# Moving the late expert-weight pieces of an audio tower: one beside each sampling chunk, sixteen into the attention's second stage

## The reference

```python
h = tok(x)                                   # 3 spliced frames -> 128 features, 166 tokens a sequence
h = h + linear_recurrence(layernorm(h))      # 256 complex states
h = h + mixture0(layernorm(h))               # 16 experts, top 2; per-expert mean of silu(x w1), then w2
h = h + sparse_attention(layernorm(h))       # 8 heads; 38 sampled keys choose 25 queries a head
h = h + mixture1(layernorm(h))               # 64 experts, top 42; gelu(x w1 + b1) w2 + b2, weighted sum
```

## Time and profile before

| | before |
|---|---|
| median of 3 runs | 2065.45 us (2064.77 to 2066.51) |
| the profiled execution | 2067.39 us |
| its span | 2065.7 us |
| PE busy | 1870.1 us (91%) |
| DVE busy | 1676.4 us (81%) |
| ACT busy | 1378.0 us (67%) |
| POOL busy | 1455.0 us (70%) |
| mean granted clock of PE | 0.939 |

### The profile page before, as it was taken

The page is one execution under the profiler, slowest core; times in us unless marked ns, Lnnn a source line. Parts: engine busy times, 40 slices in busy tenths (PEclk is TensorE's granted clock), DMA queues, the critical chain, the costliest instruction groups (busy, mean ns, idle before and its releaser), DMA issues.

```text
span 2065.7 us, 50535 instructions
## 1 busy us (share of the span) xinstructions
PE 1870.1 (91%) x17038; PEld 1349.7 (65%) x17038; DVE 1676.4 (81%) x4833; ACT 1378.0 (67%) x2149; POOL 1455.0 (70%) x1098
## 2 busy tenths in 40 slices
PE   7887436789989978999999999999999999999998
PEld 5555213456669855777777777777777777777776
DVE  5887736555678788899999999999999999999998
ACT  4134525424435545888888888888888888888886
POOL 2216679559800032888888888888888888888887
PEclk9998768789989965999999999999999999999999
DMA  3011289523200010000000200000100000000000
GB/s 93 21 35 63 81 246 257 124 67 94 90 1 1 22 63 1 2 2 0 0 0 3 82 2 0 0 0 35 49 1 0 0 0 2 2 10 11 10 11 19
DMA packets 64334, 77.56 MB, mean 38 GB/s; under 512 B 38932, under 2 KB 47028, under 8 KB 62132
## 3 DMA queue, kind: packets, MB, share of 16 engines
q1 hardware_dynamic: 61364, 70.08, 11.7%
q0 software_dynamic: 2816, 5.45, 0.8%
HBM read 42.97 MB, written 24.08 MB: 32 GB/s over the span
## 4 chain that ended last, share of the span: by engine, by line
PE 58%; DVE 3%; issue 2%; ACT 1%; POOL 0%; ACTq 0%; DVEq 0%; POOLq 0%
PE bank L2679 30%; PE bank L2662 28%; DVE m_work L2553 1%; DVE m_best L2550 1%; DVE m_work L2544 0%; PE bank L2632 0%; DVE m_ut L1269 0%; ACT m_h L2485 0%; DVE m_best L2543 0%; DVE m_ex L2555 0%; DVE h L2591 0%; DVE m_red L2556 0%; DVE m_row L2536 0%; POOL m_diag L1255 0%; ACT m_hidden L2482 0%
## 5 line engine op out<-in xcount | busy, mean ns | idle before, releaser
L2679 PEld LDWEIGHTS bank<-weights,m_h 128*128 128x128 f16 x10752 | 649.6, 98 | 194.4 <-DVE hc L2582 82.6
L2430 POOL TENSOR_TENSOR m_h<-m_hidden,m_h 128x896 f16<-128x896 f32 x384 | 725.9, 1890 | 32.0
L2679 PE MATMUL bank<-weights,m_h 128*128 128x128 f16 x10752 | 724.6, 219 | 10.7 <-POOL m_h L2430 2.1
L2582 DVE SCALAR_TENSOR_TENSOR hc<-bank,m_shares,hc 128x128 f32<-128x128 f32 x2688 | 727.2, 342 | 4.3 <-PE bank L2679 4.3
L2482 ACT ACTIVATE m_hidden<-bank,m_b 128x896 f32<-128x896 f32 x384 | 386.9, 1007 | 197.6 <-PE bank L2662 197.5
L2567 DVE TENSOR_TENSOR m_h<-bank,m_h 128x896 f16<-128x896 f32 x384 | 419.2, 1092 | 116.8 <-ACT m_h L2485 116.7
L2428 POOL TENSOR_SCALAR m_h<-m_hidden 128x896 f16<-128x896 f32 x384 | 360.8, 939 | 117.9 <-ACT m_hidden L2482 99.5
L2662 PE MATMUL bank<-m_u_first,weights 128*128 128x448 f16 (+1 forms) x1536 | 417.8, 354 | 5.5 <-DVE h L2591 5.5
L2662 PE MATMUL bank<-m_u_second,weights 128*128 128x448 f16 (+1 forms) x1536 | 417.7, 354 | 0.0
L2479 ACT ACTIVATE bank<-bank,m_b 128x896 f32<-128x896 f32 x384 | 377.6, 983 | 0.6 <-PE bank L2662 0.6
L2485 ACT ACTIVATE m_h<-bank 128x896 f16<-128x896 f32 x384 | 349.1, 909 | 0.0
(11 more groups left out here) (359 smaller groups left out, 2153.9 us busy)
## 6 DMA issues: line engine op xcount, KB each, us to landing
weights<-expert_factors SPq DMA_DIRECT2D x12, 1024.0 KB, 8.8
lru_w_in<-e_w_dram SPq DMA_DIRECT2D x16, 512.0 KB, 4.5
expert_factors<-lru_w_out SPq DMA_DIRECT2D x16, 512.0 KB, 4.3
ew_raw<-e_w_dram SPq DMA_DIRECT2D x16, 512.0 KB, 3.9
weights<-w_dram SPq DMA_DIRECT2D x16, 256.0 KB, 2.8
weights<-w_dram SPq DMA_DIRECT2D x4, 1024.0 KB, 6.6
expert_factors<-ew_made SPq DMA_DIRECT2D x8, 512.0 KB, 3.0
xs<-x_dram SPq DMA_DIRECT2D x4, 996.0 KB, 11.8
```

What stands on the lines that cost most here:

```text
L2430: g.tensor_tensor(h1[:, x, 1], hidden[:, x], h1[:, x, 0], ALU.subtract).then_inc(second_of[1], 1)
L2582: last = v.scalar_tensor_tensor(acc[:, m * TW:(m + 1) * TW], y[q][:, (n - start) * TW:(n - start + 1) * TW], shares[:, m, e:e + 1], acc[:, ...
L2679: last = t.matmul(y[q][:, (n - start) * TW:(n - start + 1) * TW], factors[:, m, n * TW:(n + 1) * TW], k.weights[:, grp % 2, 2 + m, at], st ...
```

## The change

All 32 pieces go to `ExpertWeights`; `LateWeights` is gone, and with it its SP and POOL instructions in the tiles, its 16 loads and 16 stores there, and its semaphores. The two small sums of the first mixture (`hsum`, `ym`) move to the front of their room.

- Pieces 0 to 15 stand in the first attention stage: piece c-1 after diagonal c for c = 1 to 15, and piece 15 after them, ahead of POOL's constants for the second stage. Nothing stands ahead of the first diagonal.
- Pieces 16 to 31 stand in `attend`, where SP and POOL get instructions: SP loads and stores, POOL 64 operations. SP's last wait for the stores moves there.

```diff
@@ FirstMixture
-        late.sync_load(sp, 0)
-        late.sync_load(sp, 1)
...
-            if j >= self.KEEP_FROM and (j - self.KEEP_FROM) % self.KEEP_EVERY in (0, 2):
-                late.sync_keep(sp)
-        while late.kept < late.count:
-            late.sync_keep(sp)
-        late.sync_kept(sp)
...
-    def pool(self, pool):
-        for i in range(self.late.count):
-            self.late.pool_piece(pool, i)
@@ sparse_attention, first stage
-                k.expert_weights.sync_pieces(sp, *PIECES_N3)
                 k.expert_weights.sync_pieces(sp, *PIECES_SAMPLE)
...
-                k.expert_weights.pool_pieces(pool, *PIECES_N3)
                 first, end = PIECES_SAMPLE
                 for c in range(NC):
                     norm.pool_diagonal(pool, c, c % 2, stats)
-                    if 1 <= c <= end - first:
+                    if c:
                         k.expert_weights.pool_pieces(pool, first + c - 1, first + c)
+                k.expert_weights.pool_pieces(pool, first + NC - 1, end)
@@ attend
+        @block.sync
+        def _(sp):
+            k.expert_weights.sync_pieces(sp, *PIECES_ATTEND)
+
+        @block.gpsimd
+        def _(pool):
+            k.expert_weights.pool_pieces(pool, *PIECES_ATTEND)
+
@@ constants and ExpertWeights.sync_pieces
-PIECES_N3, PIECES_SAMPLE, PIECES_SENDING = (0, 3), (3, 2 * GROUP), (2 * GROUP, NG * GROUP)
+PIECES_SAMPLE, PIECES_ATTEND = (0, 2 * GROUP), (2 * GROUP, NG * GROUP)
...
-        if end == 2 * GROUP:
+        if end == NG * GROUP:
             for p in range(2):
-                sp.wait_ge(self.k.kept_out[p], 16 * GROUP // 2)
+                sp.wait_ge(self.k.kept_out[p], 16 * (NG - 1) * GROUP // 2)
```

More of the change, by code:

```diff
@@ L937, in recurrence @@
         routing.begin(ctx, on_diag[:], tables.work[:], va[:], raw_room)
-        mixture = FirstMixture(nc, k, routing, w_in[:], w_out[:], ut[:], state_of[:], xc[:], xsn[:])
+        mixture = FirstMixture(nc, k, routing, ut[:], state_of[:], xc[:], xsn[:])
         diag_ready = sem("diag_ready")
@@ L992, in _ @@
             mixture.pool_clear(pool)
-            mixture.pool(pool)
         @block.scalar
@@ L1281, with __init__ @@
     W2_AT = (3, 8, 13)
-    KEEP_FROM, KEEP_EVERY = 4, 5
-    def __init__(self, nc, k, routing, w_in, w_out, ut, state_of, xc, xsn):
+    def __init__(self, nc, k, routing, ut, state_of, xc, xsn):
         def sem(name):
@@ L1289, in __init__ @@
         states = state_of.rearrange("p a b c d e -> p (a b c d e)")
[L1290 to L1294, removed]
+        self.hsum = states[:, 0:FC * E0 * E0].rearrange("p (f x) -> p f x", f=FC)
+        self.ym = states[:, FC * E0 * E0:FC * E0 * E0 + 128]
         self.part = xc.rearrange("p q c -> p (q c)")[:, 0:NST * FC].rearrange("p (n f) -> p n f", f=FC)
@@ L1329, in sync @@
     def sync(self, sp, outputs_made):
-        k, routing, late = self.k, self.routing, self.late
+        k, routing = self.k, self.routing
         sp.wait_ge(outputs_made, NC)
-        late.sync_load(sp, 0)
-        late.sync_load(sp, 1)
         sp.wait_ge(k.w0_split, NC)
@@ L2210, in pool_pieces @@
             g.tensor_tensor(out[:, 1], left, out[:, 0], ALU.add).then_inc(self.split, 1)
[L2215 to L2264, removed]
-            pool.wait_ge(self.kept_out[j], 16 * (i // 2))
-        g.tensor_copy(out[:, 0], raw).then_inc(self.rounded, 1)
-        pool.wait_ge(self.rounded, i + 1)
-        if i:
-            pool.wait_ge(self.split, i)
-        g.tensor_tensor(left, raw, out[:, 0], ALU.subtract).then_inc(self.raw_read, 1)
-        pool.wait_ge(self.raw_read, i + 1)
-        g.tensor_scalar(left, left, 1.0 / SHARE, 1.0, ALU.mult, ALU.mult).then_inc(self.widened, 1)
-        pool.wait_ge(self.widened, i + 1)
-        g.tensor_tensor(out[:, 1], left, out[:, 0], ALU.add).then_inc(self.split, 1)
```

## The result

The changed kernel takes 2071.87 us, the median of 15 runs (2066.66 to 2076.78). The kernel before takes 2064.43 us (15 runs, 2062.63 to 2066.96). The ratio is 1.0033, with a 95% interval of 1.0022 to 1.0043: slower, by 7.4 us. That is a third of a per cent, clear of the noise by its interval. The forecast was 2078.

What follows compares the result with a forecast made beforehand. POOL was taken to pace the tiles through SP's waits, PE to bound the sampling and be fullest in the attention's second stage. 2067.4 - 25 - 10 + 48 = 2080.4, less 1.9 for the median: 2078 us, range 2060 to 2098.

Steps and rivals of the forecast that it cites:

- The tiles, -25: First mixture's tiles: without SP's waits for POOL, DVE becomes the limit; 25 us less, bounds 0 and -36.
- The third norm, -10: Third norm and sampling: PE's wait for the first diagonal, DVE's waits and the low clock go; -10 us, bounds -5 and -12.
- The 3 us for the clock: Third norm: at full clock PE's 11.0 busy us shrink by some 4, of which ACT's copies give back 1.
- Sampling, 0: Sampling chunks: PE covers the pieces; DVE's numbering of heads meets POOL at work, 0 to 3 us, taken as 0.
- The second stage, +48: Attention's second stage: DVE waits for POOL's operations, steps of 6.85 us instead of 3.7; +48 us, bounds +40 and +60.
- the 0.06 us for each of four holds: Second stage: DVE's holds add about 0.06 us to each of four POOL operations, making a 6.6 us piece 6.85.
- A step that starts otherwise falls into that order: Second stage: steps settle with POOL's long operations in DVE's gaps, so four operations, one piece, go with each step.
- The second mixture as long as before: Second mixture: its length was expected to stay unchanged, 0 us.
- the threshold of 5.3 us a step: Second stage: below 5.3 us a step beside POOL, the loss would be under the 35 us gained elsewhere, making the kernel faster.
- the pairs do not pass together: Rival, second stage: DVE keeps the port through each pair, steps of 4.4 us, +22 us, 2052 in all; chance 0.08.
- the stage does not hide POOL: Rival, second stage: PE is fullest and DVE's idle time hides POOL, so only gains remain, 2030 us; chance 0.04.
- the tiles gained: Answers a rival: big loads or a cold PE hold the tiles at 2.6 us each, 2103 us; chance 0.08.

Runs made afterwards that it cites:

- twin without POOL's operations: Changed kernel without POOL's 64 operations on the pieces in the attention's second stage, SP's loads and stores kept: 2029.29 us, ratio 0.9856.
- three kernels with padding: Kernel before with one, two or four small unused POOL memsets more at the second mixture's start: 2052.77, 2053.28 and 2066.83 us.
- the halved operations: Changed kernel with each POOL operation on a piece in the attention's second stage cut into two of half the columns: 2067.79 us, ratio 1.0033.
- the merged comparison: Changed kernel with the two DVE comparisons that make oh written as one instruction over both halves: 2072.41 us, ratio 1.0042.

## Why the prediction was right, point by point

- **The tiles, -25: -23.1 to -23.5.** The step held as written: SP without waits for POOL, DVE the limit, two gaps at the register loads.
- **The third norm, -10: -9.4, by a slightly other sum.** The wait of 4.96 us went. DVE's waits beside POOL were worth more than the 2 us given: the first spread came 31.7 us earlier, 23.1 of them from the tiles, so 8.6 for both. DVE's busy time between its first instruction of the norm and that spread fell from 16.3 to 11.2 us. The 3 us for the clock hardly came: 0.67 instead of 0.60, and 0.8 us.
- **Sampling, 0: +4.5.** The step "DVE's numbering of the first half of the heads now meets POOL at work: 0 to 3 us, taken as 0" was mis-sized. It weighed POOL's pieces and left out the longest operation of POOL's in that stretch, the select of 4.14 us of the earlier trace rows, which ended at 545.3 as the sum there gives (570 less the 25 of the tiles) and met a cast. The size hangs on timing: in two of the eight profiles with the pieces moved and the constants behind them the cast missed the select, and the sampling took 127.5 us, as before.
- **The second stage, +48: +45.1** against before, +47 against its twin without POOL's operations. A step took 6.54 us instead of 6.85: the 0.06 us for each of four holds did not add up, since POOL's operations followed each other at their own pace. "A step that starts otherwise falls into that order" is what the steps after 11.79 us show. The page "SBUF — State Buffer" of the Trainium skill, section "Who interferes with whom", has whole instructions excluding each other; the trace agrees (1.46 and 2.54 us, each ending within 0.2 us behind an operation of POOL).
- **"The second mixture as long as before": 13.6 us shorter.** This is the step that failed, and the reason why the time came out at 2072 and not at 2085. It was taken from there being no edit in that stage. The three kernels with padding show that the code ahead of POOL's loop alone is worth 11 to 12 us, in the kernel before too. The moves themselves cost 18.1 us by the profiles, and that the time shows less than half of it is luck: the loop could as well have kept its rhythm, or lost one. The time would have been slower than before, and in the stated range, either way.

The terms' errors are +1.9, +0.6, +4.5, -2.9, +1.0 and -13.6; with the 2080.4 of the sum they give the profiled 2071.9. Without the last one the sum would have been 5.1 us too low; with it, it is 8.5 too high. Two sums beside the forecast do not come out. "By its own bounds the forecast gives 2064 to 2096" is not what the bounds add up to: 2065 - 36 - 12 + 0 + 40 is 2057, and 2065 + 0 - 5 + 3 + 60 is 2123. And the threshold of 5.3 us a step, below which the kernel would be faster, leaves out the long steps at the start: the halved operations gave steps of 5.47 us, and the stage still lost 43.0 us, 8 more than the 35 gained elsewhere. The rivals: the pairs do not pass together (steps of 6.54 us, not 4.4), the stage does not hide POOL, and the tiles gained.

## What to carry to other kernels

Before POOL work is moved to a stage where POOL is idle, count DVE's instructions there that read two SBUF tensors or rescale SBUF into SBUF. Here, with three or four of them to a step, each waited for a POOL operation, and a step became as long as POOL's round. The reductions of the tiles, which read PSUM, were no longer beside POOL than without it (0.950 and 0.948 us in the mean), and most of what looked like POOL's price there was the place of its stores in SP's queue. And compare the longest loop's rhythm whenever code ahead of it changes: a move can be credited or charged with 13 us that a single empty instruction gives as well.

## What the runs showed that I had not expected

- A POOL loop of 192 rounds costs 0.07 us a round more or less by how many instructions stand ahead of it: 0 and 4 more are slow (1227.7, 1227.4 us), 1 and 2 fast (1215.4, 1214.3). What does it is open.
- DVE and POOL do not always alternate. The cast that started at 540.73 us, while POOL did two short selects to 541.18, was not let in between them and the next: it ended only behind the select of 4.13 us that came after.
- A `tensor_scalar` of POOL on 128x1024 took 1.25 us instead of 1.04 beside the merged comparison, and a piece 6.75 instead of 6.55: DVE holds POOL up too.
- Single executions of several kernels ran 16 to 22 us above their median (2062.6, 2044.97, 2078.94, 2087.08), and two of the kernel before 17 (2081.77, 2081.81). The one whose profile was caught had PE at a clock of 0.52 over the third norm's statistics, with PE 99% busy.
